# An attention and ternary feed-forward block: the first batch's work divided anew between VectorE, ScalarE and GpSimd

## The reference

```
xn = layernorm(x)
q, k, v = mlp(xn)                      # each: gelu(xn @ W1 + b1) @ W2 + b2, 256 -> 256 -> 256
s = layernorm((tril(q @ k.T) / scale) @ v) * ln_w + ln_b
Wq = clip(round(W / (mean(|W|) + 1e-5)), -1, 1)      # ternary, both FFN matrices
g = silu(relu(xn @ Wq1.T + b1) @ Wq2.T + b2)         # 256 -> 1024 -> 256
out = x + s * g
```

## Time and profile before

| | |
|---|---|
| median of 3 runs | 322.7 us (322.67 to 324.15) |
| profiled execution | 322.39 us, its span 320.7 us |
| mean granted TensorE clock | 0.984 |
| busy, share of the span | PE 96%, VectorE 75%, ScalarE 72%, GpSimd 42% |

### The profile page before, as it was taken

How to read it: one execution, slowest core, us unless ns; L and a number is a source line. 1 busy time by engine, 2 the same in 40 slices (tenths; PEclk the granted TensorE clock), 3 DMA queues, 4 the chain that set the end, 5 groups by cost and what they waited for, 6 DMA issues and landing times. The chain is left out here.

```text
span 320.7 us, 5784 instructions
## 1 busy us (share of the span) xinstructions
PE 308.6 (96%) x1850; PEld 274.2 (86%) x1850; DVE 240.6 (75%) x552; ACT 230.2 (72%) x424; POOL 133.6 (42%) x111
## 2 busy tenths in 40 slices
PE   7997899999999999999999999999999999999992
PEld 6875699879997899888998899888998799988992
DVE  3789967788759777797768887697777887586684
ACT  2999444998469963898549973799548984599433
POOL 2033734444281733426263542618245342700254
PEclk9997799999999999999999999999999999999997
DMA  7942530310005000320003200130003100010001
GB/s 243 372 163 95 179 133 0 131 68 0 3 2 175 20 0 0 131 66 0 0 0 131 65 0 0 65 132 0 0 0 131 66 0 0 1 65 1 0 0 65
DMA packets 15769, 20.07 MB, mean 63 GB/s; under 512 B 1936, under 2 KB 12688, under 8 KB 15760
## 3 DMA queue, kind: packets, MB, share of 16 engines
q1 hardware_dynamic: 15056, 19.04, 17.4%
q10 hardware_dynamic: 704, 0.93, 0.8%
HBM read 15.74 MB, written 4.22 MB: 62 GB/s over the span
## 5 line engine op out<-in xcount | busy, mean ns | idle before, releaser
L563 DVE TENSOR_TENSOR r_lo<-bank,r_hi 128x512 fp32r<-128x512 f32 x64 | 42.5, 688 | 17.0 <-ACT bank L385 17.0
L384 ACT ACTIVATE r_hi<-bank,col 128x512 fp32r<-128x512 f32 x64 | 48.6, 759 | 0.0
L385 ACT ACTIVATE bank<-bank,col 128x512 f32<-128x512 f32 x64 | 47.1, 736 | 0.0
L295 POOL TENSOR_TENSOR y<-y,row 128x512 f32<-128x512 f32 (+1 forms) x17 | 20.9, 1231 | 52.2 <-DVE gw L590 52.1
L708 PE MATMUL bank<-xT_lo,w1q 128*128 128x512 f32 x128 | 41.1, 402 | 0.0
L708 PE MATMUL bank<-xT_hi,w1q 128*128 128x512 f32 x128 | 41.0, 402 | 0.0
L288 POOL TENSOR_TENSOR v_lo<-v,v_hi 128x1024 fp32r<-128x1024 f32 x8 | 19.2, 2402 | 48.3 <-ACT v_hi L395 48.3
L279 POOL TENSOR_TENSOR y<-y,xn 128x512 f32<-128x512 f32 x14 | 23.3, 1665 | 37.1 <-DMA xn<-x_norm_rows 37.1
L708 PE MATMUL bank<-w2q,r_lo 128*128 128x256 f32 x256 | 35.8, 281 | 0.0
L399 ACT ACTIVATE y<-y 128x512 f32<-128x512 f32 (+1 forms) x17 | 10.3, 608 | 35.4 <-DVE y L581 35.4
L708 PE MATMUL bank<-w2q,r_hi 128*128 128x256 f32 x256 | 35.3, 279 | 0.0
(11 more groups left out here) (117 smaller groups left out, 701.4 us busy)
## 6 DMA issues: line engine op xcount, KB each, us to landing
out<-x_all SPq DMA_DIRECT2D x15, 256.0 KB, 2.4
x_all<-in_x SPq DMA_DIRECT2D x7, 512.0 KB, 3.6
y<-in_x_t SPq DMA_DIRECT2D x7, 512.0 KB, 3.3
xn<-x_norm_rows SPq DMA_DIRECT2D x7, 512.0 KB, 3.5
x_all<-in_w1t SPq DMA_DIRECT2D x1, 1024.0 KB, 7.3
x_all<-in_w2t SPq DMA_DIRECT2D x1, 1024.0 KB, 11.4
row<-in_rows ACTq DMA_DIRECT2D x1, 512.0 KB, 6.8
x_all<-in_x SPq DMA_DIRECT2D x1, 256.0 KB, 3.1
```

The source lines that it names most:

```text
L295: nc.gpsimd.tensor_tensor(y[:, part], y[:, part], row[:, ROW_LNB:ROW_LNB + 1].broadcast_to((P, tiles, C)), ALU.mult).then_inc(gb_part, 1)
L384: nc.scalar.activation(r["hi"][:, f], pre[:], ACT.Relu, bias=b1)
L385: nc.scalar.activation(pre[:], pre[:], ACT.Relu, bias=b1).then_inc(f1_whole, 1)
L563: nc.vector.tensor_tensor(r["lo"][:, f], bank[(AT_F1 + f) % BANKS][:], r["hi"][:, f].bitcast(FP32), ALU.subtract).then_inc(r_split, 1)
```

## The change

All of it lies ahead of and in batch 0; the loops over the later batches keep their instructions.

- Statistics, reciprocal roots and row normalisation of x(0) go by half of the rows, each with semaphores of its own.
- W2q is loaded into a tile with one column more, into which ScalarE writes the bias b2q. The fold product takes 257 columns, and so gives the folded bias along. Its first half stands ahead of the transposes of x(0), the second behind them, each with a bank of its own. The other bias products move behind the fourth product of layer 1.
- The gelu table is loaded at the start, by a gelu of one element. ScalarE also makes `ones_r`.
- |W1| is summed by VectorE (one reduction of 2048 elements), |W2| by ScalarE as before, but one gelu later and behind the shifts of W2v.
- W1k is split by GpSimd, no more by ScalarE and VectorE.
- W1 is quantised in two halves by columns; PE's first four ternary products wait for the first half alone.
- PE adds the sums of |W1| after the third product of layer 1 and those of |W2| after the second ternary product, where it waits for two g_lo instead of six.
- W2: VectorE quantises one half, in its queue behind r_lo 1. GpSimd quantises the other: two compares with a column and a subtraction, in its queue ahead of the reciprocal roots of x(1).
- The statistics of x(1) stand behind r_lo 4 instead of ahead of the quantisation, and e_hi and e_lo behind r_lo 7.

The diff, cut:

```diff
+            for h in range(2):
+                half = slice(2 * h, 2 * h + 2)
+                pool.wait_ge(x0_var_made[h], 1)
+                nc.gpsimd.tensor_tensor(x_rstd[:, half], x_var[:, half], neg_half[:, half],
+                                        ALU.pow).then_inc(x0_rstd_made[h], 1)
+            pool.wait_ge(xn_made, TT)
+            pool.wait_ge(qkv_loaded[1], 16)
+            nc.gpsimd.tensor_copy(w["hi"][:, 1], raw_qkv[:, 1]).then_inc(wk_hi_made, 1)
+            pool.wait_ge(wk_hi_made, 1)
+            nc.gpsimd.tensor_tensor(w["lo"][:, 1], raw_qkv[:, 1], w["hi"][:, 1].bitcast(FP32),
+                                    ALU.subtract).then_inc(wk_split, 1)
...
+            def quantise_rest():
+
+                rest = slice(FT // 2, FT)
+                pool.wait_ge(thr_made, 4)
+                nc.gpsimd.tensor_scalar(less, raw2[:, rest], neg_thr[:, 1:2], None, ALU.is_lt).then_inc(less_made, 1)
+                nc.gpsimd.tensor_scalar(w2q[:, rest], raw2[:, rest], thr[:, 1:2], None, ALU.is_gt).then_inc(more_made, 1)
+                pool.wait_ge(less_made, 1)
+                pool.wait_ge(more_made, 1)
+                nc.gpsimd.tensor_tensor(w2q[:, rest], w2q[:, rest].bitcast(FP32), less,
+                                        ALU.subtract).then_inc(w2_rest_quantized, 1)
+
+            quantise_rest()
...
+            act.wait_ge(consts_made, 5)
+            nc.scalar.activation(v_shift[:, 0:1], eps[:], ACT.Gelu).then_inc(gelu_loaded, 1)
+            nc.scalar.copy(ones_r[:], ones[:]).then_inc(ones_rounded, 1)
+            act.wait_ge(cols_loaded, 16)
+            nc.scalar.copy(w2q_raw[:, :, C], col[:, COL_B2:COL_B2 + CK]).then_inc(b2q_beside, 1)
...
             weight_hi(0, 0)
-            weight_hi(1, 1)
...
-            nc.scalar.copy(w["hi"][:, 3].rearrange("p k c -> p (k c)"), bank[6][:]).then_inc(fold_hi_made, 1)
-            abs_sum_of(0, raw1, raw1_loaded)
+            for n in range(CK):
+                nc.scalar.copy(w["hi"][:, 3, n], FOLD[n][:, 0:C]).then_inc(fold_hi_made, 1)
             weight_hi(2, 2)
-            act.wait_ge(cols_loaded, 16)
...
-                    if first and m == 2:
-                        abs_sum_of(1, raw2, raw2_loaded)
+                    if first and m == 3:
                         v_shifts()
+                        abs_sum2()
...
+            def x_statistics0():
+
+                for h in range(2):
+                    dve.wait_ge(x0_loaded[h], 16)
+                    for t in (2 * h, 2 * h + 1):
+                        nc.vector.bn_stats(x_stats[:, t], x_all[:, 0, t]).then_inc(x0_stats_made[h], 1)
+                    aggregate(x_stats, x_part, x_mean, x_var, x0_stats_made[h], 2, x0_var_made[h],
+                              slice(2 * h, 2 * h + 2))
...
+            def quantise2():
+
+                dve.wait_ge(thr_made, 4)
+                dve.wait_ge(w1_quantized, 2)
+                quantise(raw2[:, 0:FT // 2], w2q[:, 0:FT // 2], 1, flags.rearrange("p (f c) -> p f c", c=C),
+                         w2_quantized, 3)
...
+            dve.wait_ge(raw1_loaded, 16)
+            nc.vector.tensor_reduce(abs_sum[:, 0:1], raw1.rearrange("p a b -> p (a b)"), mybir.AxisListType.X, ALU.add,
+                                    apply_absolute_value=True).then_inc(abs1_summed, 1)
+            for n in range(CK):
+                dve.wait_ge(fold_hi_made, n + 1)
+                nc.vector.tensor_tensor(w["lo"][:, 3, n], FOLD[n][:, 0:C], w["hi"][:, 3, n].bitcast(FP32),
+                                        ALU.subtract).then_inc(fold_read, 1)
+                nc.vector.tensor_copy(d_weight[:, n:n + 1], FOLD[n][:, C:C + 1]).then_inc(fold_read, 1)
+            split_weight(2, 2)
+            thresholds(0)
+            dve.wait_ge(thr_made, 2)
+            quantise1(0)
             dve.wait_ge(folded, 2)
             nc.vector.tensor_copy(z_bias[:], FOLD_Z)
-            nc.vector.tensor_copy(d_const[:], FOLD_D)
-            nc.vector.tensor_copy(d_weight[:], FOLD_DW).then_inc(fold_read, 1)
+            nc.vector.tensor_copy(d_const[:], FOLD_D).then_inc(bias_read, 1)
+            dve.wait_ge(w1_quantized, 1)
+            quantise1(1)
...
-                if first:
-                    x_statistics(1, second=True)
-                dve.wait_ge(e_made, i + 1)
-                nc.vector.tensor_copy(e["hi"][:], e32[:]).then_inc(e_hi_made, 1)
-                dve.wait_ge(e_hi_made, i + 1)
-                nc.vector.tensor_tensor(e["lo"][:], e32[:], e["hi"][:].bitcast(FP32), ALU.subtract).then_inc(e_split, 1)
-                if first:
-                    thresholds(1, GAMMA[1])
-                    quantise(1, raw2, w2q[:].rearrange("p a b -> p (a b)"), w2_quantized)
+                def e_parts():
+                    dve.wait_ge(e_made, i + 1)
+                    nc.vector.tensor_copy(e["hi"][:], e32[:]).then_inc(e_hi_made, 1)
+                    dve.wait_ge(e_hi_made, i + 1)
+                    nc.vector.tensor_tensor(e["lo"][:], e32[:], e["hi"][:].bitcast(FP32), ALU.subtract).then_inc(e_split, 1)
+
+                if not first:
+                    e_parts()
                 for f in range(FT):
+                    if first and f == 2:
+                        quantise2()
+                    if first and f == 5:
+                        x_statistics(1, second=True)
                     dve.wait_ge(f1_whole, 8 * i + f + 1)
                     nc.vector.tensor_tensor(r["lo"][:, f], bank[(AT_F1 + f) % BANKS][:], r["hi"][:, f].bitcast(FP32),
                                             ALU.subtract).then_inc(r_split, 1)
+                if first:
+                    e_parts()
...
-            w2qT, w2kT = raw_qkv[:, 3], raw_qkv[:, 4]
+            w2qT, w2kT = w2q_raw, raw_qkv[:, 4]
             b2q, b2k = col[:, COL_B2:COL_B2 + CK], col[:, COL_B2 + CK:COL_B2 + 2 * CK]
 
-            def fold_weights():
-
-                for n in (3, 4):
-                    pe.wait_ge(qkv_loaded[n], 16)
+            def fold_weights(n):
+
+                return split_product(FOLD[n][:, 0:C + 1],
+                                     [(w2kT[:, k, n * P:(n + 1) * P], w2qT[:, k]) for k in range(CK)])
...
-                    if first:
-                        pe.wait_ge(w_split, m // 2 + 1)
+                    if first and m % 2 == 0:
+                        pe.wait_ge(*((w_split, 1), (wk_split, 1), (w_split, 2))[m // 2])
+                    if first and m == 4:
+                        pe.wait_ge(thr_made, 2)
+                    if first and m == 5:
+                        pe.wait_ge(bias_read, 1)
                     dst = claim(i, AT_L1 + m, first)
                     h = slice((m % 2) * P, (m % 2 + 1) * P)
                     split_product(dst[:], [(w[a][:, m // 2, k, h], xT[b][:, k])
                                            for a, b in FULL for k in range(CK)],
                                   (xT_split, 2 * i + 2) if m == 0 else None).then_inc(l1_summed, 1)
-                    if first and m == 1:
-                        sum_partitions(0)
+                    if first and m == 2:
+                        sum_partitions(0, abs1_summed)
                     if first and m == 3:
-                        pe.wait_ge(thr_made, 2)
-                if first:
-                    pe.wait_ge(fold_read, 2)
-                    pe.wait_ge(w1_quantized, 2)
+                        fold_biases()
...
+                    if first and f % (FT // 2) == 0:
+                        pe.wait_ge(w1_quantized, 2 * f // FT + 1)
+                    if first and f == 0:
+                        pe.wait_ge(fold_read, 2 * CK)
+                    if first and f == 2:
+                        pe.wait_ge(g_split, 2)
+                        sum_partitions(1, abs2_summed)
+                    if first and f == 3:
                         pe.wait_ge(thr_made, 4)
...
+            pe.wait_ge(qkv_loaded[3], 16)
+            pe.wait_ge(qkv_loaded[4], 16)
+            pe.wait_ge(b2q_beside, 1)
+            fold_weights(0)
+            transpose_x0(range(TT))
+            fold_weights(1).then_inc(folded, 1)
```

More of the change, by code:

```diff
@@ L136, in gated_block @@
             sem("x_stats_made"), sem("x_var_made"), sem("x_rstd_made"), sem("xn_made"))
+        x0_stats_made, x0_var_made, x0_rstd_made = (
+            [sem(f"{n}{h}") for h in range(2)] for n in ("x0_stats_made", "x0_var_made", "x0_rstd_made"))
+        b2q_beside, wk_hi_made, wk_split, bias_read = (
+            sem("b2q_beside"), sem("wk_hi_made"), sem("wk_split"), sem("bias_read"))
+        less_made, more_made, w2_rest_quantized = sem("less_made"), sem("more_made"), sem("w2_rest_quantized")
         xT_summed, l1_summed, f1_summed, z_summed, d_summed, v_summed, y_summed, s_summed, o_summed = (
@@ L386, in batch @@
                 if first:
[L387 removed]
+                    act.wait_ge(bias_read, 1)
                 for k in range(CK):
@@ L475, in xT_lo, with thresholds @@
                                             ALU.subtract).then_inc(xT_split, 1)
```

(39 more changed lines are left out.)

107 lines of the change are left out of this document (40 added, 67 removed).

## The result

The changed kernel takes 324.96 us (median of 21 runs), the old one beside it on the same chip 323.05 (21 runs). The ratio is 1.0054 with a 95% interval of 1.004 to 1.0069: slower by 0.54%, some 1.8 us, with an interval that reaches to both sides of the 0.5% that I had called the least that can be told from no change. I had forecast slower, and 4.3 us of it. The profiled execution took 323.7 us, 1.3 less than the median of its kernel, and has a span of 321.9 us, 1.2 more than before: what follows explains these 1.2 us, and what the median has beyond them no trace shows.

What follows compares the result with a forecast made beforehand. PE's own work was taken to bound batches 2 to 8, so only batch 2's start counted: output product +3.1, second tile +0.6 and clock +0.6 made 4.3 us, giving 327.0 us on the median, range 321.8 to 330.5.

Steps and rivals of the forecast that it cites:

- The bound and the start: Batches 2 to 8 are PE's own work, 36.92 us each; layer 1 starts at about 10.0, the fold product at 27.7.
- It cannot keep that: PE, 5.9 us ahead at the fold product, loses this because batch 2 needs x(1), whose statistics now come later.
- GpSimd takes its second compare until 31.75, and VectorE's other pass waits for that and ends at 33.0: In W2's quantisation, the two engines exclude each other; VectorE's second pass waits out GpSimd's whole compare.
- cost nothing: SP's loads of x(4) onwards start behind the chain's own transfer as before, at no cost.
- my 50.6: End of GpSimd's fourth normalising step of x(1), where the old end was 40.59.
- 55.9: Start of PE's first output product, moved from 52.73 by the late chain of x(1): +3.1 us.
- The clock, +0.6: After about 4 us of idle PE the clock falls, costing 1.7; half of the 1.1 not already covered is counted.
- The second output tile: The output product's second tile waits for the next s_lo: +0.6 us.
- My rival of cheap compares: GpSimd's W2 compares take 1.2 to 1.9 us each, VectorE is held up 2 us; total 324.3, chance 0.18.
- my 3.3: Time in us of one 1024-element GpSimd compare in W2's quantisation, taken from its adds of a column to 256 elements.
- my two marks: Forecast wrong if x(1)'s statistics end before 33 or PE idles under 2 us ahead of the first output product.

Runs made afterwards that it cites:

- b1: The old kernel with only the statistics of x(1) moved behind r_lo 4 on VectorE; 329.18 us, ratio 1.0177 to the old kernel.
- a2: The changed kernel with x(1)'s statistics ahead of r_lo 0 and its roots ahead of GpSimd's half of W2; two sets, 320.91 and 321.56 us.
- a4: The changed kernel with SP waiting for the spread statistics to land before loading x(4) to x(7); 324.28 us, ratio 1.0016 to the old kernel.
- a6: a2 with both parts of e moved ahead of r_lo 5 on VectorE; 320.0 us, ratio 0.9897 to the old kernel.
- a7: The changed kernel with only the two parts of e moved ahead of r_lo 5; 325.02 us, ratio 1.0033 to the old kernel.
- a8: a6 with the magnitude sum of W1 taken back from VectorE to ScalarE; 319.82 us, ratio 0.9871 to the old kernel.
- a1: The changed kernel with only the statistics of x(1) moved ahead of r_lo 0 on VectorE; 324.84 us, ratio 1.0025 to the old kernel.
- a3: The changed kernel with VectorE quantising both halves of W2 and GpSimd none; 325.56 us, ratio 1.0069 to the old kernel.
- a5: a3 with the statistics of x(1) back ahead of r_lo 0 on VectorE; 322.05 us, ratio 0.9954 to the old kernel.

## Why the prediction came out as it did

**The bound and the start: right.** Batches 2 to 8 are unchanged to the 36.92; the first layer came at 10.03 (10.0), W1's sum took 2.28 (2.2), W1 was quantised at 19.6 (19.6), the fold product came at 27.78 (27.7), the layer of relus ended at 32.1 (31.8).

**"It cannot keep that": right.** b1 shows that the late statistics alone cost the old kernel 1.8% (2.9 us of it in the slow stretch behind the product), a2 that early statistics and roots turn the change into a gain. PE's 5.9 us were given back to a wait on the chain of x(1).

**The step that failed: "GpSimd takes its second compare until 31.75, and VectorE's other pass waits for that and ends at 33.0".** It ended at 29.72. I had taken from one subtraction of VectorE beside two-tensor operations of GpSimd that any pass of VectorE over two SBUF operands waits for any GpSimd instruction. The runs show three cases, with 1.28 us for the pass alone:

| VectorE's pass over W2 | GpSimd beside it | us |
|---|---|---|
| the change, a2 twice, a4, a6, a7, a8 | column compare | 2.02 |
| a1 | subtraction of two tensors | 3.28 |
| a3, a5 | nothing | 1.28 |

Beside the compare it takes 0.74 more and is over some 0.7 us before the compare is (29.72 and 30.40 in the change). Nor does it lengthen the compare: in a2 the first compare is 0.55 longer than the second, about what VectorE's own compare, over at 29.1, still had to run. In all seven traces the pass begins 0.04 us after VectorE's own compare has ended, and so just when GpSimd's compare, held up by that, gets going; no run has a pass that begins in the midst of a GpSimd compare. a1 has small operations in both places: x_var, at the beginning of the second compare, took 1.03 us instead of 0.16, while x_part<-x_stats, also of two SBUF operands, took its ordinary 0.17 two us into the first. So the 0.74 may be a price of the compare's beginning alone; this is not shown for the pass. VectorE's column compare (0.75 us, where the pass over as many elements takes 1.28) is the case that I had right: in the change it started at 26.06, ended at 27.66, 0.54 after GpSimd's compare, and GpSimd's next was 0.43 longer. The Trainium skill ("SBUF — State Buffer", Who interferes with whom) has a full block until the other's end in each of these; by it the pass in the change would have ended at 31.7 by my estimate, 1.28 behind GpSimd's compare at 30.40. The traces agree for VectorE's column compare and for GpSimd's subtraction, and speak against it for this pair. The pass took 2.02 us where I had 4.5 from 28.5 to 33.0; with 0.85 less for VectorE's compare ahead of it, since GpSimd's compare began and ended earlier than I had it, this is the 3.4 us by which the statistics came early.

**"cost nothing": wrong as well.** I had SP's loads of x(4) behind the chain's transfer "as before". They were issued 0.82 us behind it instead of 2.72, and the transfer took 1.3 us longer; a4 gives 1.1 to 1.2 of it back. This error and the first went opposite ways, so that the time came nearer to the forecast by luck: statistics 3.4 early, but the end of normalising at 47.98 only 2.6 before my 50.6, and the product at 53.31 instead of 55.9.

**The clock, +0.6: not paid in the profiled execution, though the fall came.** It fell behind the 3.02 us that PE waited for e_lo. The slow stretch (7.06 us) was over at 43.66, and PE, done with its work at 51.42, still had 1.89 us to wait for the output product's operand: the fall was covered. In b1 and a7 the long wait stood ahead of the output product, and there the stretch behind was 2.9 and 3.1 us longer than its 3.56. That an idle time of 2.5 us is followed by a fall I had from one row; in b1 one of 2.55 ahead of the fold product was followed by 4.1 us at 1.00, and the two profiles of a2 differ likewise. The second output tile waited, as forecast: 0.35 for its operand and 0.69 in the stretch (4.25 instead of 3.56).

The sum of these: 4.3, less 2.6 for the product and 0.6 for the clock, is 1.1, where batch 2 shows 1.27. The medians are 1.9 apart; the rest is in no trace, since the change's profile is of an execution faster than its median. My rival of cheap compares had nearly this time, 324.3, by another cause: the compares did take 2.86 us each alone, near my 3.3 and far from 1.2 to 1.9. Of my two marks one held (the statistics not before 33: they came at 33.64), and the other, an idle time of no less than 2 us, failed with 1.89.

## What to carry to other kernels

Before work is moved ahead in one queue, find the chain that leaves from what it is moved ahead of, with its store, its load and its steps on a slow engine, and compare its end with where the main engine will then be: here 6 us gained on TensorE in the first products were worth nothing until the statistics of x(1) and the roots stood first in both queues; then the same parts gave 0.6 to 1.1% in the two sets of a2. When an instruction is shared out between VectorE and GpSimd, price each pair that will run side by side by its own row, compare beside pass (0.74 us more here) and subtraction beside pass (2.0 more). And a load that a moved wait sets free can run into the very transfer that is now critical.

## What the hardware showed that I had not expected

- VectorE's pass of two SBUF operands takes 2.02 us beside a column compare of GpSimd that sets out with it and 3.28 beside a subtraction of two tensors, 1.28 alone. With one operand in PSUM (r_lo) it is not held: the six r_lo of a2 that ran beside GpSimd's compares took 3.67 us, and three in the change, from 29.64 on, in part beside its subtraction, 1.87, some 0.6 each, as ever.
- Small instructions are held as well: in a1 the four-element x_var, beside a compare, took 1.03 us instead of 0.16, and the roots, beside VectorE's pass, 2.03 instead of 1.04.
- A GpSimd compare of a 128x1024 tensor with a column takes 2.86 us alone, less than the 3.3 that 0.92 for 256 elements had led me to; the two shifts of 128x256 took 2.60 beside VectorE's quantisation of W1 instead of 1.84.
- A fall of the clock cost nothing in the change, where a wait followed it, and 2.9 and 3.1 us in b1 and a7, where none did. Idle times of 2.94 and 2.96 us in two executions of a2 were followed by the full clock in one and by a fall in the other.
